# Two slots for the result instead of four, and a fourth chunk of slack in X and Y: a two-layer cross-head convolution on one Trainium2 core

## The chip, the cores and the metric

The kernel runs on one core of a Trainium2 chip. The metric is device time in microseconds of one execution, the median of several runs. The trace shows TensorE (PE, its weight loads as PEld), VectorE (DVE), ScalarE (ACT), GpSimd (POOL), SyncE (SP), which issues all DMAs here, and the DMA engines.

## The reference

```python
def layer(x, w, qw1, qw2, kw1, kw2, qdd, kdd):      # x: (1, 16, 1024, 1024), channels M, rows T, columns S
    ret = einsum('BGMTS,GMN->BGNTS', x, w + eye(16))
    ret += einsum('BGITS,BTGIM->BGMTS', einsum('BGMTS,BTGIM->BGITS', x, qw1), qw2)   # rank 2, by row t
    ret += einsum('BGITS,BSGIM->BGMTS', einsum('BGMTS,BSGIM->BGITS', x, kw1), kw2)   # rank 2, by column s
    return ret + x * qdd[by row] + x * kdd[by column]
out = layer(layer(x, *L0), *L1)
```

All is float32. At each point (t, s) the 16 channels are multiplied by a 16 x 16 matrix R[t] that depends on the row and by another C[s] that depends on the column, and the two products are added; this is done twice.

## The kernel before

**Layout.** The 1024 rows are cut into 8 blocks of 128 rows. A block of x lies on chip in X: a partition holds one channel of one eighth of the columns, and in it 64 pairs of rows by 128 columns by 2. Y is a second buffer of the same shape for what is between. A block is moved in 16 chunks of 8 rows, 512 KB each. X and Y are longer than a block by SLACK = 3 chunks: the blocks lie alternately at the start and at the end of the buffer (`pair_place`), so that the first three chunks of the next block (`pair_at`) have a place of their own, and each further chunk j of it takes the place of chunk j of the block before. OUT holds OUT_SLOTS = 4 chunks of the result.

**Matrices.** 16 x 16 matrices are spread to block-diagonal weights: those of rows from RT, of columns from RS. GpSimd makes all of WA and the odd groups of WB, VectorE the even groups of WB, each SLOTS = 4 groups ahead. The column matrices are made once at the start (`fill` on TensorE brings the factors to all partitions, `column_unit` on VectorE multiplies and adds). Their factors wait in KR: those of layer 0 in OUT, those of layer 1 in the slack of Y and X, one half each. The row matrices of the next block are made by VectorE in the T pass (`products_of`, at step PROD_STEP = 6), stored by SyncE (`store_products`, PROD_STORE = 9) and read back, broadcast, into RT.

**Passes.** Block k goes through an S pass and a T pass.

- S pass: TensorE multiplies by the column matrices, `s1` for layer 0 (out of X into the banks PB, which VectorE adds into Y: `add_columns`), `s2` for layer 1 (out of Y into PA, which ScalarE copies to X). VectorE starts an S pass only when ScalarE's copies of the T pass before are complete.
- T pass: for each of 16 steps o, TensorE multiplies a chunk of Y by the row matrices of layer 1 (`t2`, two groups, into PB) and then a chunk of the next block's x by the row matrices of layer 0 (`t1(k + 1, o)`, into PA, copied to Y by ScalarE). VectorE adds the part of PB and of X into OUT (`add_rows`, two a chunk, the first waits for the slot's last store), makes an even group of WB between the two adds, and makes the products behind step 6. `t2` takes the chunks in the order SLACK, SLACK + 1, ..., the first SLACK chunks last. The last block has no `t1`.

**Order on SyncE.** In a T pass it waits at each step for both adds, stores the chunk, and issues `load_x(k + 1, o + SLACK)`, whose place is now free. At step 9 it then stores the products (two DMAs) and loads the row parameters of the block after (`load_q`), before it comes to the store of step 10. The first SLACK chunks of a block are loaded at the start of the S pass before, ahead of the two loads of RT.

TensorE's `t1(k + 1, o)` needs chunk o of x landed; `t2` of group g needs the adds of group g - 4 (four banks PB) and its weights.

Of the kernel before, what the change touches and what calls it, by code (L numbers as in the profile page):

```python
# [10 lines left out]
EIGHTHS = HALVES * PARTS  # L11
# [4 lines left out]
RANK = 2  # L16
LAYERS = 2
PAIR = 2
PAIRS = ROWS // PAIR
CHUNK = 8  # L20
CHUNKS = ROWS // CHUNK
CHUNK2 = CHUNK // PAIR
SLACK = 3
NARROW = 4
GROUPS = WIDE // NARROW
INDEX = HALVES * NARROW
# [3 lines left out]
T2_GROUPS = ROWS // FEW  # L30
RING = 2
SLOTS = 4
OUT_SLOTS = 4
LAG = 2
QUARTERS = 4
QUARTER = COLS // QUARTERS
UNITS = LAYERS * QUARTERS * RANK
FILLS = 4
# [4 lines left out]
DMA = 16  # L43
FLAT = CHUNK * COLS
BANK = 512
# [5 lines left out]
def cross_conv_kernel(nc, x, first_rows, row_params, col_left, col_right, w, products, out):  # L51
# [13 lines left out]
    with ctx:  # L65
        def sb(name, shape):
            return ctx.enter_context(nc.sbuf_tensor(name, shape, f32))

        def sem(name):
            return ctx.enter_context(nc.semaphore(name))  # L70

        ALL = PAIRS + SLACK * CHUNK2
        X = sb("X", [P, ALL, COLS, PAIR])
        Y = sb("Y", [P, ALL, COLS, PAIR])
        OUT = sb("OUT", [P, OUT_SLOTS, CHUNK2, COLS, PAIR])
        RT = sb("RT", [P, LAYERS, ROWS, CH])
# [20 lines left out]
        sel = later[:, at:at + P]  # L97

        VALUES = RANK * COLS * CH
        KR = [[OUT[0:EIGHTHS, :, :, :, :].rearrange("q a b c d -> q (a b c d)")[:, 0:VALUES]],  # L100
              [buf[0:EIGHTHS, PAIRS:ALL, :, :].rearrange("q a b c -> q (a b c)")[:, 0:VALUES // 2]
               for buf in (Y, X)]]


        PA = [ctx.enter_context(nc.psum_tensor(f"PA{i}", [P, BANK], f32)) for i in range(RING * HALVES)]
        PB = [ctx.enter_context(nc.psum_tensor(f"PB{i}", [P, BANK], f32)) for i in range(RING * HALVES)]
# [1 line left out]
        x_loaded = [sem(f"x_loaded{j}") for j in range(CHUNKS)]  # L108
        first_loaded = sem("first_loaded")
        left_loaded = sem("left_loaded")  # L110
        right_loaded = [sem(f"right_loaded{h}") for h in range(3)]
        q_loaded = sem("q_loaded")
        ident_step = sem("ident_step")
        ident_ready = sem("ident_ready")
# [20 lines left out]
        b_done = sem("b_done")  # L135
        stored = [sem(f"stored{n}") for n in range(OUT_SLOTS)]

# [10 lines left out]
        def t2_groups(k):  # L148
            return (GROUPS + T2_GROUPS) * k + GROUPS
# [18 lines left out]
        def pair_place(k):  # L168
            return SLACK * CHUNK2 * (k % 2)

        def pair_at(k, j):

            if j >= SLACK:
                return CHUNK2 * j
            return CHUNK2 * j + PAIRS * (k % 2)

        def t2_chunk(o):
            return (o + SLACK) % CHUNKS

        def first(k):  # L180
            return isinstance(k, int) and k == 0
# [39 lines left out]
        def _(sp):  # L221
            def load_x(k, j):
                sp.dma_start(rows_of(X, k, j).rearrange("q a s c -> q (a s c)"),
                             x[bass.ds(k * CHUNKS + j, 1)].rearrange("b q v -> (b q) v")).then_inc(x_loaded[j], DMA)

            def store(k, o):
                sp.dma_start(out[bass.ds(k * CHUNKS + t2_chunk(o), 1)].rearrange("b q v -> (b q) v"),
                             OUT[:, o % OUT_SLOTS].rearrange("q a s c -> q (a s c)")
                             ).then_inc(stored[o % OUT_SLOTS], DMA)

            def load_right(l, h, signal):
                n = VALUES // len(KR[l])
                sp.dma_start(KR[l][h], col_right[l, :, n * h:n * (h + 1)]).then_inc(signal, DMA)

            def load_q(step):
                sp.dma_start(QP[:, :, :].rearrange("q l v -> q (l v)"),
                             row_params[bass.ds(step, 1)].rearrange("b t v -> (b t) v")).then_inc(q_loaded, DMA)

            def store_products(place, src, signal):
                sp.dma_start(products[bass.ds(place, 1)].rearrange("b c t n -> (b t) c n"), src).then_inc(signal, DMA)  # L240
# [7 lines left out]
            def s_phase(k, more):  # L248
                if more:
                    if not first(k):  # L250
                        sp.wait_ge(b_done, s1_done(k))
                    else:
                        sp.wait_ge(right_done, UNITS)
                    for j in range(SLACK):
                        load_x(k + 1, j)
# [13 lines left out]
            def t_phase(k, more, params):  # L269
                for o in range(CHUNKS):  # L270
                    sp.wait_ge(b_done, t2_done(k) + PER_CHUNK * (o + 1))
                    store(k, o)
                    if more and o + SLACK < CHUNKS:
                        load_x(k + 1, o + SLACK)
# [5 lines left out]
                            load_q(k + 2)  # L280

            sp.dma_start(QF, first_rows).then_inc(first_loaded, DMA)
            load_right(0, 0, right_loaded[0])
            sp.dma_start(KL.rearrange("q l i s -> q (l i s)"), col_left).then_inc(left_loaded, DMA)
            sp.dma_start(WI.rearrange("q l n -> q (l n)"),
                         w.unsqueeze(0).broadcast_to([EIGHTHS, CH, LAYERS * CH])).then_inc(left_loaded, DMA)
            load_x(0, 0)
            sp.wait_ge(first_prod, 1)
            store_products(BLOCKS * LAYERS, PF[:, 0], first_stored)
            for h in range(2):  # L290
                load_right(1, h, right_loaded[1 + h])
            load_q(0)
            load_x(0, 1)
            sp.wait_ge(first_stored, DMA)
# [18 lines left out]
            for slot in stored:  # L313
                sp.wait_ge(slot, DMA * BLOCKS * CHUNKS // OUT_SLOTS)

# [124 lines left out]
        def _(dve):  # L440
# [73 lines left out]
            def add_rows(k, g):  # L514
                o, inner = g // PER_CHUNK, FEW2 * (g % PER_CHUNK)
                dve.wait_ge(b_full, t2_groups(k) + g + 1)
                if g % PER_CHUNK == 0 and not (first(k) and o < OUT_SLOTS):

# [55 lines left out]
        def _(pe):  # L574
# [10 lines left out]
            def fill(u):  # L585

                l, place = u // (QUARTERS * RANK), u % (QUARTERS * RANK)
                per = QUARTERS * RANK // len(KR[l])
                pe.wait_ge(right_loaded[l + place // per], DMA)
                if u >= FILLS:  # L590
                    pe.wait_ge(right_done, u - FILLS + 1)
                nc.tensor.matmul(PB[u % FILLS][:, :], sel[0:EIGHTHS],  # L592
                                 KR[l][place // per][:, BANK * (place % per):BANK * (place % per + 1)],
                                 start=True, stop=True).then_inc(right_full, 1)

            def t1(k, j):
# [65 lines left out]
            for u in range(FILLS):  # L662
                fill(u)
            for j in range(CHUNKS):
                t1(0, j)
                if FILLS + j < UNITS:
                    fill(FILLS + j)
# [66 lines left out]
```

## Time and profile before

| | us |
|---|---|
| median of 3 runs | 865.64 |
| lowest, highest | 861.66, 874.1 |
| the profiled execution | 858.88 |
| its span, first to last instruction | 857.1 |
| busy: TensorE, its weight loads | 766.5, 704.4 |
| busy: VectorE, GpSimd, ScalarE | 546.1, 513.6, 393.6 |
| x loads, stores of the result (512 KB each) | 128, 128 |

The profile is of one execution. An engine's busy time is the sum over its instructions; a wait is idle time of an engine, put down to what released it. Times of rows count from the span's start. The mean granted clock of TensorE was 0.976 of full speed.

### The profile page before, as it was taken

What the parts mean: (1) busy time and instruction counts of PE and PEld (TensorE: products, weight loads), DVE (VectorE), ACT (ScalarE), POOL (GpSimd) and SP (SyncE); (2) the same over time, 40 slices, a digit from 0 to 9 for tenths busy, and PEclk for the clock granted to TensorE, in tenths of its full rate; (3) what the DMA queues carried; (4) which work ended last, traced back from release to release, by engine and by line L of the source; (5) the groups of instructions that cost most, each with busy time, mean ns of one, the idle gap of its engine ahead of it and who ended that gap; (6) DMA issues with size and microseconds to landing.
All of it is one profiled execution on the core that took longest, in us unless ns stands there. A gap on an engine that the chain in (4) does not pass through costs nothing.

```text
span 857.1 us, 42054 instructions
## 1 busy us (share of the span) xinstructions
PE 766.5 (89%) x18464; PEld 704.4 (82%) x18464; DVE 546.1 (64%) x809; ACT 393.6 (46%) x673; POOL 513.6 (60%) x456
## 2 busy tenths in 40 slices
PE   5998899799898999797998899979998889988998
PEld 2658799699787988797987898868998779877997
DVE  3338557468474866665676675837758566665668
ACT  6224563247432583225833466325743267324640
POOL 2326577467665677555766567646776567765733
PEclk9999999999999999989999999999999999999999
DMA  9804318952568618774098723785167840985026
GB/s 190 296 3 100 93 59 309 295 185 66 200 213 296 180 25 293 232 282 101 3 333 237 265 75 131 277 277 183 44 245 257 297 110 6 341 251 184 4 116 278
DMA packets 76045, 157.09 MB, mean 183 GB/s; under 512 B 39768, under 2 KB 40792, under 8 KB 73944
## 3 DMA queue, kind: packets, MB, share of 16 engines
q1 hardware_dynamic: 75888, 154.61, 55.5%
q8 instruction: 146, 2.39, 1.1%
q14 instruction: 11, 0.09, 0.0%
HBM read 85.25 MB, written 69.34 MB: 180 GB/s over the span
## 4 chain that ended last, share of the span: by engine, by line
POOL 34%; PE 25%; issue 24%; DVE 7%; DMA 5%; SPq 2%; POOLq 1%; ACT 1%; DVEq 0%; ACTq 0%
POOL WA L200 19%; POOL WB L208 9%; PE PB L655 7%; PE PA L607 7%; POOL WB L200 6%; PE PA L642 5%; PE PB L624 4%; DMA X<-in_x_dram 3%; DVE OUT L524 3%; PE PB L592 3%; DVE WB L208 2%; SPq L240 1%; DVE PROD L478 1%; DMA RT<-products 1%; DVE PROD L481 1%
## 5 line engine op out<-in xcount | busy, mean ns | idle before, releaser
L524 DVE TENSOR_TENSOR OUT<-PB,X 128x512 f32<-128x512 f32 x256 | 172.4, 686 | 185.0 <-PE PB L655 141.0
L402 ACT ACTIVATE Y<-PA 128x512 f32<-128x512 f32 (+1 forms) x256 | 147.3, 634 | 306.7 <-PE PA L607 306.7
L412 ACT ACTIVATE X<-PA 64x512 f32 (+3 forms) x384 | 232.7, 606 | 118.5 <-PE PA L642 111.8
L655 PE MATMUL PB<-Y,WB 128*128 128x128 f32 x2048 | 272.6, 286 | 1.7 <-issue 1.0
L655 PEld LDWEIGHTS PB<-Y,WB 128*128 128x128 f32 x2048 | 248.8, 193 | 15.8 <-issue 6.2
L208 POOL TENSOR_TENSOR WB<-RT,mask 128x512 f32<-128x512 f32 x128 | 156.3, 1221 | 106.1 <-PE PB L655 102.6
L511 DVE TENSOR_TENSOR Y<-PB,Y 128x512 f32 (+1 forms) x256 | 164.8, 685 | 80.7 <-PE PB L624 69.5
L607 PEld LDWEIGHTS PA<-X,WA 64*64 64x64 f32 x8192 | 149.4, 145 | 78.1 <-issue 37.8
L642 PE MATMUL PA<-Y,WA 64*64 64x128 f32 x4096 | 190.9, 311 | 20.7 <-issue 14.3
L607 PE MATMUL PA<-X,WA 64*64 64x64 f32 x8192 | 170.1, 234 | 44.0 <-DMA X<-in_x_dram 25.3
L200 POOL TENSOR_TENSOR WA<-RS,mask 128x512 f32<-128x512 f32 x128 | 139.4, 1089 | 110.7 <-PE PA L642 85.4
L624 PE MATMUL PB<-X,WB 64*64 64x128 f32 x4096 | 189.1, 311 | 14.6 <-DVE Y L511 9.3
L200 POOL TENSOR_TENSOR WA<-RT,mask 128x512 f32<-128x512 f32 x128 | 140.6, 1102 | 85.4 <-PE PA L607 47.1
L642 PEld LDWEIGHTS PA<-Y,WA 64*64 64x64 f32 x4096 | 163.7, 139 | 25.7 <-issue 16.4
L624 PEld LDWEIGHTS PB<-X,WB 64*64 64x64 f32 x4096 | 162.2, 139 | 18.7 <-issue 18.4
L208 DVE TENSOR_TENSOR WB<-RT,mask 128x512 f32<-128x512 f32 x128 | 102.8, 803 | 0.0
L200 POOL TENSOR_TENSOR WB<-RS,mask 128x512 f32<-128x512 f32 x64 | 80.7, 1262 | 33.6 <-PE PB L655 16.7
L200 DVE TENSOR_TENSOR WB<-RS,mask 128x512 f32<-128x512 f32 x64 | 69.2, 1082 | 0.0
L501 DVE TENSOR_TENSOR PB<-PB,RT 128x512 f32<-128x512 f32 x16 | 11.2, 700 | 31.1 <-PE PB L592 31.0
L478 DVE TENSOR_TENSOR PROD<-QP 128x256 f32<-128x256 f32 x32 | 22.3, 735 | 0.0
L592 PE MATMUL PB<-OUT,RT 8*128 8x512 f32 x16 | 15.4, 1104 | 5.4 <-DMA OUT<-in_right_dram 5.4
L419 ACT ACTIVATE RS<-RT,delta 128x128 f32<-128x128 f32 x32 | 12.5, 574 | 4.6 <-DVE RT L559 4.6
(24 smaller groups left out, 62.4 us busy)
## 6 DMA issues: line engine op xcount, KB each, us to landing
X<-in_x_dram SPq DMA_DIRECT2D x128, 512.0 KB, 6.0
out_dram<-OUT SPq DMA_DIRECT2D x128, 512.0 KB, 4.5
RT<-products SPq DMA_DIRECT2D x15, 1024.0 KB
products<-PROD SPq DMA_DIRECT2D x16, 128.0 KB, 8.2
RT<-products SPq DMA_DIRECT2D x1, 768.0 KB
QP<-in_rows_dram SPq DMA_DIRECT2D x8, 80.0 KB, 3.5
RT<-in_left_dram SPq DMA_DIRECT2D x1, 384.0 KB
RT<-products SPq DMA_DIRECT2D x1, 256.0 KB
```

Of the source, the lines that this page charges most:

```text
L200: engine.tensor_tensor(dst.rearrange("q (t a n) -> q t a n", t=CHUNK, a=PARTS), r, m, ALU.mult).then_inc(ready, 1)
L208: engine.tensor_tensor(dst.rearrange("q (t p n) -> q t p n", t=FEW, p=EIGHTHS), r, m, ALU.mult).then_inc(ready, 1)
L402: nc.scalar.activation(rows_of(Y, k, j)[:, :, WIDE * h:WIDE * (h + 1), :].rearrange("q a s c -> q a c s"), PA[HALVES * (j % RING) + h][:, ...
L412: nc.scalar.activation(columns_of(block_of(X, k), dst, WIDE * i + NARROW * g), by_columns(PA[HALVES * (g % RING) + i][src, :]), ACT.Copy). ...
L478: nc.vector.tensor_tensor(prod[:, i], q1[i].unsqueeze(2).broadcast_to(shape), q2[i].unsqueeze(1).broadcast_to(shape), ALU.mult).then_inc(p ...
L511: nc.vector.tensor_tensor(at, by_columns(PB[HALVES * (g % RING) + h][:, :]), at, ALU.add).then_inc(b_done, 1)
L524: nc.vector.tensor_tensor(rows(OUT[:, o % OUT_SLOTS]), PB[g % SLOTS][:, :].rearrange("q (a c s) -> q a c s", a=FEW2, c=PAIR), rows(rows_of ...
L592: nc.tensor.matmul(PB[u % FILLS][:, :], sel[0:EIGHTHS], KR[l][place // per][:, BANK * (place % per):BANK * (place % per + 1)], start=True, ...
L607: last = nc.tensor.matmul(PA[HALVES * (j % RING) + h][part(o), WIDE * r:WIDE * (r + 1)], matrix(WA[:, j % SLOTS], h, r), rows_of(X, k, j)[ ...
L624: last = nc.tensor.matmul(PB[HALVES * (g % RING) + h][part(o), ROWS * v:ROWS * (v + 1)] .rearrange("q (a c) -> q a c", c=PAIR), matrix(WB[ ...
L642: last = nc.tensor.matmul(PA[HALVES * (g % RING) + i][part(h ^ i), ROWS * v:ROWS * (v + 1)] .rearrange("q (a c) -> q a c", c=PAIR), matrix ...
L655: last = nc.tensor.matmul(PB[g % SLOTS][:, COLS * r:COLS * (r + 1)], WB[:, g % SLOTS, P * r:P * (r + 1)], rows_of(Y, k, t2_chunk(o))[:, (i ...
```

## The change

SLACK goes from 3 to 4 and OUT_SLOTS from 4 to 2. So X and Y are 4 KB a partition longer each, and OUT is 8 KB shorter. Four chunks of the next block have a place of their own, and step o of a T pass loads chunk o + 4. The first add of a chunk waits for the store of two chunks before. The factors of the column matrices lie whole in the slack of X (layer 0) and of Y (layer 1) and are loaded by one DMA each.

```diff
-SLACK = 3
+SLACK = 4
...
-OUT_SLOTS = 4
+OUT_SLOTS = 2
...
-        KR = [[OUT[0:EIGHTHS, :, :, :, :].rearrange("q a b c d -> q (a b c d)")[:, 0:VALUES]],
-              [buf[0:EIGHTHS, PAIRS:ALL, :, :].rearrange("q a b c -> q (a b c)")[:, 0:VALUES // 2]
-               for buf in (Y, X)]]
+        KR = [buf[0:EIGHTHS, PAIRS:ALL, :, :].rearrange("q a b c -> q (a b c)")[:, 0:VALUES] for buf in (X, Y)]
...
-        right_loaded = [sem(f"right_loaded{h}") for h in range(3)]
+        right_loaded = [sem(f"right_loaded{l}") for l in range(LAYERS)]
...
-            def load_right(l, h, signal):
-                n = VALUES // len(KR[l])
-                sp.dma_start(KR[l][h], col_right[l, :, n * h:n * (h + 1)]).then_inc(signal, DMA)
+            def load_right(l):
+                sp.dma_start(KR[l], col_right[l]).then_inc(right_loaded[l], DMA)
...
-            load_right(0, 0, right_loaded[0])
+            load_right(0)
...
-            for h in range(2):
-                load_right(1, h, right_loaded[1 + h])
+            load_right(1)
...
-                per = QUARTERS * RANK // len(KR[l])
-                pe.wait_ge(right_loaded[l + place // per], DMA)
+                pe.wait_ge(right_loaded[l], DMA)
...
-                                 KR[l][place // per][:, BANK * (place % per):BANK * (place % per + 1)],
+                                 KR[l][:, BANK * place:BANK * (place + 1)],
```

## Rows read from the trace of the kernel before

**Rows 1.** The page: busy time of each engine, its share of the span, instructions

```profile
PE 766.5 (89%) x18464; PEld 704.4 (82%) x18464; DVE 546.1 (64%) x809; ACT 393.6 (46%) x673; POOL 513.6 (60%) x456
```

**Rows 2.** Waits, whole run: engine, line, releaser: sum in us, times, longest

```profile
DVE OUT L524 <- PE PB L655: 141.0, 75, 7.9
...
PE PA L607 <- DMA X<-in_x_dram: 25.3, 14, 4.9
```

**Rows 3.** Busy time by stretch, T(4) and T(7); last: clock, DMA share, GB/s

```profile
522.20:585.70 63.50, 54.85 (x1348) 50.98 (x1345) 37.31 (x59) 20.84 (x36) 38.85 (x34) 0.97 0.73 248
821.70:857.10 35.40, 31.20 (x260) 29.65 (x256) 29.58 (x46) 2.37 (x4) 14.84 (x14) 1.00 0.59 238
```

**Rows 4.** Timeline of PE, T(4): start, us, line, operation, count, idle before

```profile
562.11 1.17 PE L607 MATMUL PA<-X,WA 64*64 64x64 f32 x64 [0.70 <-DMA X<-in_x_dram]
...
573.65 1.50 PE L607 MATMUL PA<-X,WA 64*64 64x64 f32 x64 [3.72 <-DMA X<-in_x_dram]
575.09 3.30 PE L655 MATMUL PB<-Y,WB 128*128 128x128 f32 x16
...
585.72 1.39 PE L624 MATMUL PB<-X,WB 64*64 64x128 f32 x32 [0.81 <-DVE Y L511]
```

**Rows 5.** Timeline of PE, x waits of T(0), T(3) and T(6)

```profile
169.13 1.99 PE L607 MATMUL PA<-X,WA 64*64 64x64 f32 x64 [4.93 <-DMA X<-in_x_dram]
...
459.12 1.17 PE L607 MATMUL PA<-X,WA 64*64 64x64 f32 x64 [0.29 <-DMA X<-in_x_dram]
...
770.16 1.17 PE L607 MATMUL PA<-X,WA 64*64 64x64 f32 x64 [1.20 <-DMA X<-in_x_dram]
```

**Rows 6.** Timeline of SyncE's issues in T(4), steps 9 and 10

```profile
557.09 0.35 SPq L227 DMA_DIRECT2D out_dram<-OUT  x1
557.64 0.75 SPq L223 DMA_DIRECT2D X<-in_x_dram  x1
558.68 5.83 SPq L240 DMA_DIRECT2D products<-PROD  x2
...
566.87 0.35 SPq L227 DMA_DIRECT2D out_dram<-OUT  x1
```

**Rows 7.** Landings in T(4): store 7; store 10; load 13; stores 11 to 13

```profile
DMA to landing us min/median/max: 2.9/2.9/2.9
...
DMA to landing us min/median/max: 3.2/3.2/3.2
...
DMA to landing us min/median/max: 6.2/6.2/6.2
...
DMA to landing us min/median/max: 6.8/7.9/8.4
```

**Rows 8.** Timeline of VectorE in T(7), two weight builds two chunks apart

```profile
844.09 0.95 DVE L208 TENSOR_TENSOR WB<-RT,mask 128x512 f32<-128x512 f32 x1
...
847.99 0.95 DVE L208 TENSOR_TENSOR WB<-RT,mask 128x512 f32<-128x512 f32 x1
```

**Rows 9.** Landings of the 16 stores of T(7)

```profile
DMA to landing us min/median/max: 2.6/2.7/3.7
```

**Rows 10.** Timeline of VectorE in T(4): adds of chunks 7, 12 and 15

```profile
550.60 0.68 DVE L524 TENSOR_TENSOR OUT<-PB,X 128x512 f32<-128x512 f32 x1
...
564.53 0.69 DVE L524 TENSOR_TENSOR OUT<-PB,X 128x512 f32<-128x512 f32 x1 [2.10 <-PE PB L655]
...
581.96 0.71 DVE L524 TENSOR_TENSOR OUT<-PB,X 128x512 f32<-128x512 f32 x1
```

**Rows 11.** Landings: store 7 of T(5); stores 7 and 10 of T(6)

```profile
DMA to landing us min/median/max: 5.1/5.1/5.1
...
DMA to landing us min/median/max: 4.6/4.6/4.6
...
DMA to landing us min/median/max: 5.0/5.0/5.0
```

**Rows 12.** Landings of all 128 stores

```profile
DMA to landing us min/median/max: 2.6/4.5/10.0
```

More of the change, by code:

```diff
@@ L587, in fill @@
                 l, place = u // (QUARTERS * RANK), u % (QUARTERS * RANK)
-                per = QUARTERS * RANK // len(KR[l])
-                pe.wait_ge(right_loaded[l + place // per], DMA)
+                pe.wait_ge(right_loaded[l], DMA)
                 if u >= FILLS:
                     pe.wait_ge(right_done, u - FILLS + 1)
-                nc.tensor.matmul(PB[u % FILLS][:, :], sel[0:EIGHTHS],
-                                 KR[l][place // per][:, BANK * (place % per):BANK * (place % per + 1)],
+                nc.tensor.matmul(PB[u % FILLS][:, :], sel[0:EIGHTHS], KR[l][:, BANK * place:BANK * (place + 1)],
                                  start=True, stop=True).then_inc(right_full, 1)
```

## The prediction

> **What bounds the kernel now.** I read the page's busy shares first: TensorE is busy for 766.5 us of 857.1 [rows 1], so a change pays only where it removes idle time of TensorE, or shifts the few places where another engine ends last. The list of waits comes second. TensorE waits for loads of x for 25.3 us in 14 waits [rows 2]; that sum is what the fourth chunk of slack can address. VectorE waits 141.0 us for TensorE in the T passes [rows 2], so in general it has spare time there, and a new wait on it costs only what exceeds that.
>
> Third comes the table by stretch. I write T(k) for the T pass of block k. In T(4), 522.2 to 585.7 us, VectorE is busy 37.31 of 63.5 us and the DMA engines 0.73 [rows 3]. In the last pass, T(7), which has no next block to interleave, VectorE is busy 29.58 of 35.4 us and TensorE 31.20 [rows 3]: there the two are level and neither has room.
>
> Fourth, the timeline of TensorE. Each of T(0) to T(6) has at most two sizeable x waits: before t1 of chunk 10, 0.70 us in T(4), and before t1 of chunk 13, 3.72 us in T(4) [rows 4]; over the passes single waits run from 0.29 us (T(3), chunk 10) to 4.93 us (T(0), chunk 13) [rows 5]; the seven at chunk 10 sum to 7.1 us, the rest stands at chunk 13 and, 0.75 us in T(6), at chunk 14. After the long one the granted clock is at its lower level (1.2 instead of 2.4 GHz): the next two groups take 1.50 and 3.30 us in place of 1.17 and 2.08, 1.55 us more [rows 4].
>
> Fifth, SyncE's issues say why chunk 13. With SLACK 3, load 12 goes out behind store 9 at 557.64, then the two stores of products take SyncE's queue for 5.83 us from 558.68, and store 10, with load 13 behind it, comes at 566.87 [rows 6]. Load 13 lands 6.2 us after its issue [rows 7], some 573.6, exactly when TensorE goes on.
>
> **Part 1: four chunks of slack.** Load 10 now follows store 6 instead of store 7, so it no longer sits behind VectorE's products (step 6), and that wait goes. Load 13 now follows store 9 and goes out before the products, about 8.5 us before TensorE asks; that wait goes too. What is late next is load 14: it takes the place of load 13 behind store 10. Its landing, 6.2 us after issue, is when TensorE arrives one chunk (3.1 us) later, so a wait is left, from 0.1 us in T(4) to 1.3 us in T(0). The same 128 loads and 128 stores are made, each of 512 KB. Four of a block's loads instead of three go out at the start of its S pass, ahead of the RT loads; the DMA engines have room there, and RT is wanted tens of us later, so this costs nothing. If that cover were gone, it would be one load, about 1.5 us a block. The factors of layer 0 and 1 load into X and Y slack, as one DMA each: same bytes, and the first is waited for as before; nothing. Another order of the row chunks inside the pass changes no shape; nothing.
>
> **Part 2: two slots for OUT.** VectorE's first add of chunk o now waits for store o-2 where it waited for store o-4. Behind the waiting add stand on VectorE: the even WB weights of two chunks ahead, for which TensorE waits, then the second add, whose completion SyncE wants before store o and load o+4.
>
> In T(7) the sum is clear. VectorE spends 1.95 us a chunk (from its weight build at 844.09 to the like one at 847.99 are two chunks, 3.9 us) [rows 8]. A store lands 2.6 us after issue at the least, median 2.7, most 3.7 [rows 9]. A slot's round is then: two adds and a weight build 2.0, to the issue 0.1, landing 2.6, to the add 0.1: 4.8 us for two chunks instead of 3.9. That is 0.45 us a chunk, for 14 chunks 6.3 us; the first two stores land slower (up to 3.7), so I take **+6.5 us**, bounds 5 (some of it absorbed by what lies after the last add) and 10 (3.1 us a landing throughout). No cover exists here: the pass ends the kernel.
>
> The Trainium skill's main page, section Best Practices, says to double-buffer so that DMA and compute overlap. Taken as it stands, two slots would do and T(7) would cost nothing, the sum 6.5 us lower; the landing of 2.6 us against 1.95 us of work a chunk speaks against that. Its page "DMA: Bandwidth & Descriptors", section Anatomy of one DMA, fits about 2.0 us plus bytes over 436 GB/s per DMA (measured there on another issue path), an estimated 3.2 us for 512 KB, by which T(7) would lose 0.75 us a chunk, 10 us; the trace here has 2.6.
>
> In T(0) to T(6) I walk T(4). Chunks 0 to 6: stores land up to 6 us after issue behind the loads, so VectorE begins chunks 2 to 4 up to 2 us late, but TensorE needs the even weights only two chunks later and VectorE has 1 us spare in each chunk of 3.1; by step 6 it is level. Products occupy it until 550.60 [rows 10]. It then catches up at 2 us a chunk. Store 7 lands 2.9 us after 552.65 [rows 7], at 555.6, where the first add of chunk 9 ran at 554.9: +0.7. Store 9 and all behind it, the products too, move by 0.7: store 10 at 567.6, landed (3.2 us [rows 7]) at 570.8. Only then may chunk 12 be added (564.5 before), so the weights for t2 of chunk 14 are ready at 572.2. TensorE, without its x waits, arrives at 570.3 and waits 1.9 us. Stores 11 to 13 took 6.8 to 8.4 us [rows 7]; store 11 lands at 575.5, weights for chunk 15 at 576.9, TensorE waits another 1.4 and starts the S pass at 580.1, where it was 582.4: 2.3 us won. But VectorE's last adds hang on stores 12 and 13 (landed 578.1 and 580.7), and end at 582.7, as before (581.96 + 0.71 [rows 10]). The S pass's third group waits for VectorE's column adds, 585.72 before [rows 4]; now 584.2. So T(4) wins **1.5 us** of the 4.4 + 1.5 that stood there: the store chain replaces the load wait.
>
> The other passes go by the same steps; what differs is the landing of store 7, which sets how late chunk 9 and the products start, that of store 10, and the x wait that goes. T(6), the worst: store 7 lands 4.6 us after its issue at 751.69, chunk 9 starts 2.8 us late, store 10 moves from 763.7 to 766.4 and lands after 5.0 us [rows 11] at 771.4, weights for chunk 14 at 772.8 where t2 began at 771.3; the x wait won was only 1.20 [rows 5], and VectorE ends 2.3 us later: +2.3. T(5): store 7 lands after 5.1 us [rows 11], 2.9 us late, +1.0. T(0), the best: 0.9 us late, and 4.93 us of wait go [rows 5]; load 14 and store 13 hold the end: -2.4. Between them T(1) -0.4, T(2) +1.1 (it had no wait at chunk 13 to win) and T(3) +0.7. Sum of seven: **+0.8 us**. Bounds: -3 a pass (-21), if stores land in 2.6 us as in T(7), and +2.2 a pass (+15), if in 5 us or more.
>
> **Sum.** 0.8 + 6.5 = 7.3 us on the profiled execution's 858.88, 866.2. That execution lies 6.8 us under the median of the runs, 865.64, which I take as base: 865.64 + 7.3 = 872.9, rounded **872**.
>
> **Rivals.** (a) *Slower: the store chain rules every T pass.* Place: VectorE before the first add of chunks 9, 12 and 14. Price: if stores behind loads land in over 4.1 us (two chunks of 3.11 less 2.1 of work and issue), VectorE falls behind by half of the excess each chunk; the median over all passes is 4.5 us and the most 10.0 [rows 12]. It then reaches products late and every pass ends some 2.3 us later: 7 x 2.3 + 8 = 24, time 889. For it: the median is above the point. Against: those landings are backlog, and a later issue lands sooner. (b) *The x waits go whole and stores don't bite in the middle*: -25.3, and 6 to 7 of half clock (1.55 where it fell), + 6.5 in T(7): -25, time 841. For it: VectorE's 141.0 us of waiting. Against: store 10 is stuck behind the products whatever the slack. (c) *Two slots suffice everywhere*, the double-buffering rule: T(7) costs nothing, T passes win the 1.5 of T(4) each: -10, time 855. Against: 4.8 over 3.9 us. (d) *It doesn't do what it says*: the wait of chunk 13 moves whole to chunk 14, only chunk 10's 7 us are won: 0 with T(7), time 865.
>
> **How the numbers follow.** About 2% (17 us, 848 to 883) is what a measurement here tells from none; the runs before alone span 861.66 to 874.1. Forecast 0.55, (a) 0.18, (b) 0.05, (c) 0.10, (d) 0.12. Faster by over 2% is (b): 0.05. Slower is most of (a) and the edge of the forecast: 0.18. Within: 0.77. The range goes from (c) with 3 us of scatter, 852, to (a), 888.
>
> **What would show it.** Right: VectorE waits on "DMA out_dram<-OUT" at chunks 9, 12 and 14; T(7) longer by 6 to 7 us; TensorE's x waits under 10 us, what is left at chunk 14; TensorE waiting for WB weights of VectorE at chunk 14. Wrong: x waits of 20 us or more at chunk 14, T(7) at 31 us again, or TensorE waiting for VectorE's weights at chunks 4 to 9. Most likely cause of a miss: landings of stores when fewer loads stand before them, which no row shows.

## The result, and the profile after

The changed kernel took 883.83 us (median of 4 runs, 880.39 to 884.28) against 863.65 us before (4 runs, 856.28 to 874.1): ratio 1.0254, 95% interval 1.0178 to 1.0331. It is slower, by 20 us in the medians; whether by more than 2% the interval leaves open. The ratios and their intervals leave out runs that lie over 1.5% above the fastest of the same kernel, the medians don't (without them before has 861.66 us, and the difference is 22 us). The profiled execution has a span of 882.3 us where before had 857.1, so 25.2 us are to be found in the traces.

The list of waits of the changed kernel (engine, line, releaser: sum in us, times, longest):

```profile
DVE OUT L520 <- DMA out_dram<-OUT: 138.9, 76, 6.5
...
PE PB L649 <- DVE WB L206: 43.2, 25, 3.3
...
PE PB L618 <- DVE OUT L520: 13.9, 10, 3.5
DVE OUT L520 <- PE PB L649: 11.8, 8, 2.0
...
PE PA L601 <- DMA X<-in_x_dram: 0.5, 2, 0.3
```

The slack does what it is for: TensorE's waits for x go from 25.3 [rows 2] to 0.5 us. But VectorE, which waited 141.0 us for TensorE [rows 2], now waits 138.9 us for stores and 11.8 for TensorE: the order of who leads is turned round. What TensorE won on x it lost more than once over, 43.2 us on VectorE's weights and 13.9 on its adds.

Where the 25.2 us lie, from the timelines of TensorE (a T pass from its first t2 matmul to the first s2 matmul of the S pass behind it, an S pass from there to the next t2):

| us | before | after | difference |
|---|---|---|---|
| T(0) to T(6) | 63.9, 65.3, 63.7, 61.0, 64.6, 60.6, 59.4 = 438.5 | 60.7, 63.3, 65.4, 64.8, 63.5, 68.7, 62.6 = 449.0 | +10.5 |
| T(7), TensorE's part | 31.1 | 39.1 | +8.0 |
| seven S passes | 263.8 | 268.8 | +5.0 |
| start, and from the last matmul to the end | 119.4 + 4.2 | 119.9 + 5.6 | +1.9 |

(The first S pass lies in the start. The rows are rounded, so they sum to 25.4; T(0) to T(6) after are 448.9 unrounded.)

What fills T(0) to T(6), as sums of idle time in TensorE's timelines: waits for weights 0.7 us before and 36.6 after, for VectorE's adds into OUT 0 and 13.9, for its column adds 5.4 and 0, for x 25.3 and 0.5, and stalls of TensorE's own, which the rows call "issue", 15.3 and 5.3. The busy time is 391.7 and 392.3 us.

The timeline of TensorE in T(4) of the changed kernel:

```profile
550.96 2.08 PE L649 MATMUL PB<-Y,WB 128*128 128x128 f32 x16
552.98 1.17 PE L601 MATMUL PA<-X,WA 64*64 64x64 f32 x64
557.46 3.78 PE L649 MATMUL PB<-Y,WB 128*128 128x128 f32 x16 [3.32 <-DVE WB L206]
561.17 1.99 PE L601 MATMUL PA<-X,WA 64*64 64x64 f32 x64
...
581.45 2.08 PE L649 MATMUL PB<-Y,WB 128*128 128x128 f32 x16 [0.63 <-DVE WB L206]
583.46 1.17 PE L601 MATMUL PA<-X,WA 64*64 64x64 f32 x64
584.44 1.38 PE L618 MATMUL PB<-X,WB 64*64 64x128 f32 x32
587.16 2.59 PE L618 MATMUL PB<-X,WB 64*64 64x128 f32 x64 [1.34 <-DVE OUT L520]
```

The big wait is no longer at chunk 13 for x [rows 4] but at chunk 9 for weights, 3.32 us, and behind it the granted clock is at its lower level again (3.78 and 1.99 us where 2.08 and 1.17 stand at the upper): 2.5 us more. The wait stands at chunk 9 in T(1), T(3), T(4) and T(6) with 3.32 us each, in T(5) with 1.74: 15.0 us in five passes. VectorE in the same pass says why:

```profile
533.85 0.69 DVE L520 TENSOR_TENSOR OUT<-PB,X 128x512 f32<-128x512 f32 x1 [1.49 <-DMA out_dram<-OUT]
534.46 1.58 DVE L206 TENSOR_TENSOR WB<-RT,mask 128x512 f32<-128x512 f32 x1
...
545.32 0.69 DVE L520 TENSOR_TENSOR OUT<-PB,X 128x512 f32<-128x512 f32 x1 [2.44 <-DMA out_dram<-OUT]
...
548.75 0.69 DVE L520 TENSOR_TENSOR OUT<-PB,X 128x512 f32<-128x512 f32 x1 [1.54 <-DMA out_dram<-OUT]
...
550.55 1.98 DVE L474 TENSOR_TENSOR PROD<-QP 128x256 f32<-128x256 f32 x2
...
556.12 0.69 DVE L520 TENSOR_TENSOR OUT<-PB,X 128x512 f32<-128x512 f32 x1
556.73 0.68 DVE L206 TENSOR_TENSOR WB<-RT,mask 128x512 f32<-128x512 f32 x1
...
575.37 0.69 DVE L520 TENSOR_TENSOR OUT<-PB,X 128x512 f32<-128x512 f32 x1 [4.72 <-DMA out_dram<-OUT]
```

Chunks 2, 3, 5 and 6 wait for stores (chunk 3 for 1.62 us at 538.26), so the products begin 24.5 us into the pass (550.55 less 526.04) and end at 556.1; the weights for chunk 9 are made at 556.73 to 557.4, and TensorE, there at 554.1, goes on at 557.46. The same places in T(4) of the kernel before, which starts at 522.25, first on TensorE, then on VectorE:

```profile
538.63 0.58 PE L607 MATMUL PA<-X,WA 64*64 64x64 f32 x22 [1.00 <-issue]
...
549.06 0.45 PE L607 MATMUL PA<-X,WA 64*64 64x64 f32 x11 [0.65 <-issue]
...
552.55 2.08 PE L655 MATMUL PB<-Y,WB 128*128 128x128 f32 x16
```

```profile
545.28 1.86 DVE L478 TENSOR_TENSOR PROD<-QP 128x256 f32<-128x256 f32 x2
...
551.20 0.68 DVE L208 TENSOR_TENSOR WB<-RT,mask 128x512 f32<-128x512 f32 x1
```

There the products began 23.0 us into the pass, and the weights for chunk 9 were ready at 29.6 us (551.9), now at 31.4. TensorE comes earlier: to chunk 9 at 30.3 us before (552.55) and at 28.1 now. In one pass before, T(1), the weights of chunk 9 were late already:

```profile
251.23 2.08 PE L655 MATMUL PB<-Y,WB 128*128 128x128 f32 x16 [0.66 <-DVE WB L208]
```

Later, chunk 12 waits 4.72 us for store 10, which was again behind the products on SyncE:

```profile
563.71 0.35 SPq L225 DMA_DIRECT2D out_dram<-OUT  x1
564.25 0.35 SPq L221 DMA_DIRECT2D X<-in_x_dram  x1
564.89 4.71 SPq L237 DMA_DIRECT2D products<-PROD  x2
569.79 1.89 SPq L233 DMA_DIRECT2D QP<-in_rows_dram  x1
571.94 0.35 SPq L225 DMA_DIRECT2D out_dram<-OUT  x1
```

T(7), TensorE's timeline: what was one unbroken stretch of 31.15 us is now cut by waits for weights.

```profile
837.59 7.79 PE L649 MATMUL PB<-Y,WB 128*128 128x128 f32 x64
846.15 3.90 PE L649 MATMUL PB<-Y,WB 128*128 128x128 f32 x32 [0.78 <-DVE WB L206]
851.85 3.90 PE L649 MATMUL PB<-Y,WB 128*128 128x128 f32 x32 [1.80 <-DVE WB L206]
856.51 3.90 PE L649 MATMUL PB<-Y,WB 128*128 128x128 f32 x32 [0.76 <-DVE WB L206]
861.17 3.90 PE L649 MATMUL PB<-Y,WB 128*128 128x128 f32 x32 [0.77 <-DVE WB L206]
867.55 9.14 PE L649 MATMUL PB<-Y,WB 128*128 128x128 f32 x64 [2.48 <-DVE WB L206]
```

From 856.51 to 861.17 are two chunks, 4.66 us: the round of one slot (2.0 of work, 2.6 of landing and a little between), where two chunks of work alone are 3.9. The 8.0 us that the pass is longer are the five waits, 6.6 us in sum, and half clock behind the last of them: the four chunks from 867.55 take 9.14 us where the four from 837.59 take 7.79.

### The profile page after: what moved, and what is told of

The parts are those of the page before. It is cut to its first block, busy times and chain, and to the rows that moved or that the text cites. A ratio compares the mean times of both kernels' runs of the same rounds, so it can differ in the third digit from the quotient of the medians.

```text
span 882.3 us, 42083 instructions
## 1 busy us (share of the span) xinstructions
PE 771.3 (87%) x18464; PEld 708.1 (80%) x18464; DVE 567.1 (64%) x809; ACT 393.9 (45%) x673; POOL 512.8 (58%) x456
## 4 chain that ended last, share of the span: by engine, by line
PE 40%; DMA 19%; DVE 15%; issue 11%; POOL 6%; SPq 4%; ACT 3%; DVEq 1%; ACTq 0%; POOLq 0%
DMA out_dram<-OUT 17%; PE PB L618 13%; PE PA L636 12%; PE PB L649 7%; PE PA L601 6%; DVE OUT L520 5%; DVE WB L206 5%; POOL WA L198 4%; ACT X L408 3%; DVE PROD L474 3%; PE PB L587 3%; SPq L237 2%; POOL WB L198 2%; DVE PROD L477 1%; SPq L233 1%
## 5 line engine op out<-in xcount | busy, mean ns | idle before, releaser
L649 PE MATMUL PB<-Y,WB 128*128 128x128 f32 x2048 | 273.5, 286 | 43.4 <-DVE WB L206 43.2
L520 DVE TENSOR_TENSOR OUT<-PB,X 128x512 f32<-128x512 f32 x256 | 173.4, 686 | 194.7 <-DMA out_dram<-OUT 138.9
L206 POOL TENSOR_TENSOR WB<-RT,mask 128x512 f32<-128x512 f32 x128 | 148.7, 1162 | 128.9 <-PE PB L649 125.4
L618 PE MATMUL PB<-X,WB 64*64 64x128 f32 x4096 | 195.3, 316 | 25.5 <-DVE OUT L520 13.9
L198 POOL TENSOR_TENSOR WA<-RS,mask 128x512 f32<-128x512 f32 x128 | 143.1, 1118 | 90.0 <-PE PA L636 81.9
L618 PEld LDWEIGHTS PB<-X,WB 64*64 64x64 f32 x4096 | 168.2, 143 | 30.5 <-issue 26.8
L636 PEld LDWEIGHTS PA<-Y,WA 64*64 64x64 f32 x4096 | 167.5, 141 | 26.0 <-issue 16.7
L198 POOL TENSOR_TENSOR WA<-RT,mask 128x512 f32<-128x512 f32 x128 | 144.6, 1134 | 74.1 <-PE PA L601 33.4
L206 DVE TENSOR_TENSOR WB<-RT,mask 128x512 f32<-128x512 f32 x128 | 117.6, 919 | 0.0
L474 DVE TENSOR_TENSOR PROD<-QP 128x256 f32<-128x256 f32 x32 | 27.2, 891 | 0.0
L587 PE MATMUL PB<-X,RT 8*128 8x512 f32 x16 | 15.4, 1104 | 5.3 <-DMA X<-in_right_dram 5.3
L587 PE MATMUL PB<-Y,RT 8*128 8x512 f32 x16 | 16.5, 1136 | 0.0
```

Of the source, the lines that this page charges most:

```text
L198: engine.tensor_tensor(dst.rearrange("q (t a n) -> q t a n", t=CHUNK, a=PARTS), r, m, ALU.mult).then_inc(ready, 1)
L206: engine.tensor_tensor(dst.rearrange("q (t p n) -> q t p n", t=FEW, p=EIGHTHS), r, m, ALU.mult).then_inc(ready, 1)
L474: nc.vector.tensor_tensor(prod[:, i], q1[i].unsqueeze(2).broadcast_to(shape), q2[i].unsqueeze(1).broadcast_to(shape), ALU.mult).then_inc(p ...
L520: nc.vector.tensor_tensor(rows(OUT[:, o % OUT_SLOTS]), PB[g % SLOTS][:, :].rearrange("q (a c s) -> q a c s", a=FEW2, c=PAIR), rows(rows_of ...
L587: nc.tensor.matmul(PB[u % FILLS][:, :], sel[0:EIGHTHS], KR[l][:, BANK * place:BANK * (place + 1)], start=True, stop=True).then_inc(right_f ...
L618: last = nc.tensor.matmul(PB[HALVES * (g % RING) + h][part(o), ROWS * v:ROWS * (v + 1)] .rearrange("q (a c) -> q a c", c=PAIR), matrix(WB[ ...
```

## The experiments

Each time below is a median; the kernel before ran beside each experiment, with medians of 861.5 to 863.0 us. All edits are given against the kernel named.

**The four corners: two slots alone, slack alone.** The first leaves SLACK at 3 and uses two of the four slots; the kernel before with:

```diff
-OUT_SLOTS = 4
+OUT_SLOTS = 2
...
-        OUT = sb("OUT", [P, OUT_SLOTS, CHUNK2, COLS, PAIR])
+        OUT = sb("OUT", [P, 2 * OUT_SLOTS, CHUNK2, COLS, PAIR])
```

> SLACK stays 3, only two of the four OUT slots are used. Theory (store chain): the last pass grows from 31.1 to about 39 us as in the changed kernel, the passes with a next block keep their waits for x (20 us or more, since load 13 is still behind the products) and get the waits for weights on top, so the kernel is slower than the changed one: 885 to 900 us. Rival (the four chunks of slack cost, for example by more loads in the S pass): two slots alone cost only the last pass, 870 to 875 us.

893.72 us, ratio 1.0404 (1.0347 to 1.046). As the theory had it. Its waits for stores, x and weights:

```profile
DVE OUT L524 <- DMA out_dram<-OUT: 139.3, 78, 5.3
...
PE PA L607 <- DMA X<-in_x_dram: 39.0, 20, 5.5
...
PE PB L655 <- DVE WB L208: 19.9, 12, 3.3
```

The waits for x grow from 25.3 to 39.0 (by the order on SyncE a later add makes a later load), and 19.9 for weights come on top. T(7) is 38.3 us.

The second has both, SLACK 4 and four slots, on the changed kernel, with the room taken from RS:

```diff
-OUT_SLOTS = 2
+OUT_SLOTS = 4
...
-        RS = sb("RS", [P, LAYERS, COLS, CH])
+        RS = sb("RS", [P, 1, COLS, CH])
```

and all uses of `RS[:, 0]` and `RS[:, 1]` on that one half (ScalarE's base for layer 1 goes to the still unused OUT).

> SLACK 4 with four OUT slots; the room comes from RS, of which both layers use one half, so the column matrices of the second layer are not its own (same instructions, another result). Theory: waits for x fall from 25.3 to under 10 us (left at chunk 14, behind the products), the last pass is 31 us again, time 840 to 852 us. Rival (the slack is worth nothing, because the wait moves whole to chunk 14): x waits 18 us or more, time 855 to 865 us.

844.99 us, ratio 0.9833 (0.9779 to 0.9887). Waits for x:

```profile
PE PA L603 <- DMA X<-in_x_dram: 8.0, 6, 1.9
...
PE PB L651 <- DVE WB L206: 3.5, 6, 0.7
```

The time and the waits are as the theory had them. T(7) is 31.15 us again, T(0) to T(6) sum to 419.3. So with four slots the slack wins 16.5 us and with two 9.9 (893.72 less 883.83), while the two slots cost 32 with SLACK 3 and 39 with SLACK 4. The change is a win of some 10 to 16 us bought with 32 to 39.

**The products later on SyncE's queue.** One constant, on the kernel before (to 12) and on the changed one (to 15):

```diff
-PROD_STORE = 9
+PROD_STORE = 12
```

> The kernel before, with the two stores of products and the load of row parameters behind step 12 instead of 9, when all loads of x of the pass are out. Theory (SyncE's queue, held by the products, makes load 13 late): the waits for x at chunk 13 go, those at chunk 10 (7 us in sum) stay, time 840 to 852 us. Rival (the transfers themselves are late because the DMA engines are full): waits for x stay at 20 us or more, time 858 to 868 us.

> The changed kernel, with the stores of products behind step 15 instead of 9. Theory (in the passes with a next block, part of the loss is the store of chunk 10 held behind the products, then chunks 12 and 14): the waits of TensorE for weights late in the pass shrink, those at chunk 9 stay, the last pass stays at 39 us; time 866 to 876 us. Rival (two slots lag by themselves, whatever stands on SyncE's queue): 880 to 886 us.

841.3 us, ratio 0.9796 (0.9728 to 0.9863), and 863.7 us, ratio to before 1.005 (0.9986 to 1.0115): 20 us each. The first one's waits for x, and then the changed kernel's waits with the same edit:

```profile
PE PA L607 <- DMA X<-in_x_dram: 7.5, 9, 1.5
```

```profile
DVE OUT L520 <- DMA out_dram<-OUT: 105.4, 80, 3.2
...
PE PB L649 <- DVE WB L206: 25.3, 18, 3.3
```

So what made load 13 late was SyncE's queue, not full DMA engines: no x wait at chunk 13 is left, and the 7.5 us stand at chunks 10 and 11. One constant wins as much as the fourth chunk of slack (20 against 16.5 us, a difference within the intervals). In the changed kernel the same edit takes 18 of the 43 us of weight waits, mostly late in the passes; the 3.3 us at chunk 9 stay in four passes (243.61, 445.04, 542.49, 742.43 us in its timeline), T(7) is 37.8. The time, 863.7 us, is a little under what was expected.

**Both on the slack.** The kernel with SLACK 4 and four slots, PROD_STORE 12:

> SLACK 4, four OUT slots (both layers again on one half of RS, so another result) and the stores of products behind step 12. Theory (the slack is worth what load 13 and load 10 gain; late products alone already free load 13): only the chunk 10 wait of some 7 us is left for the slack to win over late products alone (841.3), time 832 to 838 us, x waits under 2 us. Rival (slack and late products add in full, -16.5 and -20): 825 us.

837.89 us, ratio 0.9673 (0.9583 to 0.9762). TensorE waits for x no more. Against late products alone, 841.3, the slack is worth 3 us, within the intervals of both: the two remedies treat the same wait and do not add.

**Four slots in the last pass alone.** The changed kernel; in T(7) chunks 2 and 3 of every four use X's free slack (the adds, the stores and their waits all go by `slot`):

```diff
+        def slot(k, o):
+            if last(k) and o % 4 >= 2:
+                n = o % 4 - 2
+                return X[:, CHUNK2 * n:CHUNK2 * (n + 1)], spare_stored[n]
+            return OUT[:, o % OUT_SLOTS], stored[o % OUT_SLOTS]
```

> The changed kernel, where the last pass alone takes two more slots, in the slack of X that no load uses then. Theory (a slot's round of work, issue and landing sets the last pass): it falls from 39.1 to 31 us, time 875 to 877 us. Rival (the last pass is longer for another reason, such as VectorE's slower weight builds beside GpSimd): it stays over 36 us, time 882 us or more.

878.16 us, ratio 1.0148 (1.007 to 1.0226). The time is a little over the 875 to 877 us of the theory. The last pass of it, one row again:

```profile
842.23 31.15 PE L664 MATMUL PB<-Y,WB 128*128 128x128 f32 x256
```

So the slots are the whole of the 8.0 us there. They are also the 1.4 us from the last matmul to the end, which is 4.2 us again: 9.4 us by the traces. The medians differ by 5.7; in the profiled pair T(0) to T(6) are as long (448.5 and 448.9 us) and the S passes 5.0 us longer, which is their scatter (below).

**The products in two pieces on VectorE.** On the kernel before with PROD_STORE 12, and, in steps 3 and 6 with the stores left behind step 9, on the changed one:

```diff
-                    if more and o == PROD_STEP:
-                        products_of(k + 1)
+                    if more and o in (3, 7):
+                        products_of(k + 1, ((0,), (1,))[o == 7])
```

> The kernel before with the stores of products behind step 12, and VectorE's products cut in two, layer 0 behind step 3 and layer 1 behind step 7. Theory (the remaining 7.5 us of x waits at chunk 10 come from VectorE being held 5.4 us in one piece behind step 6): they fall under 2 us, time 832 to 837 us. Rival (they come from the landing of loads under full DMA engines): unchanged, 841 us.

> The changed kernel with VectorE's products cut in two, layer 0 behind step 3 and layer 1 behind step 6, stores as before behind step 9. Theory (with two slots VectorE comes late into the products, so that the weights of chunk 9 are late, 15.7 us of TensorE's wait over the passes plus half clock): those waits halve or go, time 868 to 876 us. Rival (the lag is only moved, each piece of products meets the store chain): 880 us or more.

829.76 us, ratio 0.9609 (0.9536 to 0.9682): waits for x 1.4 us, and a time under what was expected; the waits at chunks 10 and 11 did come from VectorE being held in one piece behind step 6. And 871.18 us, ratio 1.0107 (1.0064 to 1.015), 12.7 under the changed kernel. The time is as the theory said, and so are the waits at chunk 9, which fall from 15.0 to 4.1 us. But others come in their place, as the rival had it, and the sum of all waits for weights hardly falls from 43.2:

```profile
PE PB L649 <- DVE WB L206: 41.9, 34, 4.4
```

There are now more and shorter ones (34 in place of 25), most of them of 0.6 to 0.8 us; the long ones left stand at chunk 14 (4.37 us in T(4)). T(0) to T(6) sum to 436.9, not 448.9; TensorE is busy in them for 384.7 us, not 392.3, and the mean granted clock of the run is 0.976, not 0.964. So some 7 of the 12 us are half clock that stood behind long waits. The sum of waits is not the price: one wait of 3.32 us with 2.5 us of half clock behind it costs more than five of 0.65.

**All on the changed kernel.** Late and split products; then also four slots in T(7); then also the fourth x load of an S pass late in it:

```diff
-                    for j in range(SLACK):
+                    for j in range(SLACK - 1):
...
+                    sp.wait_ge(a_full, s2_groups(k) + 10)
+                    load_x(k + 1, SLACK - 1)
```

> The changed kernel with both: products of VectorE in two pieces (steps 3 and 6) and their stores behind step 15. Theory (in the passes with a next block the two slots cost time mainly where they meet the products, on VectorE and on SyncE's queue): the weight waits of those passes fall from 36.6 to under 12 us, the last pass stays near 38; time 850 to 856 us. Rival (two slots cost as much without the products): 862 us as with late stores alone.

> As the run before, and the last pass with two more slots in free slack. Theory (the parts add): 6 to 8 us less than the run before, 843 to 849 us, still over the kernel before with late and split products (829.8), since the slack then has little to win. Rival (the slack wins 10 us once nothing else holds the pass): 830 us or less.

> As the run with all three edits on the changed kernel (late and split products, four slots in the last pass), but of the four loads of x at the start of an S pass the fourth goes out late in that pass, behind ten of its sixteen groups. Theory (the fourth load beside the loads of RT lengthens TensorE's stalls on its own instruction fetch, so that the seven S passes sum to 267 to 281 us with SLACK 4 against 260 to 270 with SLACK 3): the sum falls to 270 or less, time 826 to 831 us. Rival (those sums differ by chance or for another reason): 274 us or more, time as before, 835.

849.74 us, ratio 0.9767 (0.9685 to 0.9849); 834.82 us, ratio 0.9646 (0.9581 to 0.9711); 835.32 us, ratio 0.9612 (0.9558 to 0.9665). One run of the last took 3443 us; that isn't explained.

The first is just under its range. Its weight waits are 16.3 us, 4.1 of them in T(7), so 12.2 in the other passes where under 12 were expected. T(0) to T(6) sum to 412.8 us there and, with the same code for these passes, to 406.0 in the second; four slots with late and split products have 405.3. So away from the products two slots cost these passes little, at most the 7 us by which the two traces differ.

The second came 15 us under the first by the medians, where 6 to 8 were expected, and under its range. But these medians have few runs that scatter: by the runs that the ratios count (838.36 and 847.07 us; 827.18, 834.27 and 835.38) they are 842.7 and 834.3, which is 8.4 us apart. The edit itself explains 7.9 by the traces: T(7) is 31.15 in place of 37.6, and from the last matmul to the end it is 4.2 in place of 5.6. The third tests a guess on the S passes: their sum is 280.3 us, as without the edit (281.4), and the time is as before; the theory falls.

**The best version once more.**

> Four slots, SLACK 3, products in two pieces (steps 3 and 7) and stored behind step 12, once more with more rounds: 826 to 834 us, 3 to 5% under the kernel before.

830.28 us, ratio 0.9652 (0.9598 to 0.9705), 6 runs: four slots, SLACK 3, products in two pieces and stored late. It has run twice, at 829.76 and 830.28. The changed kernel with all remedies, 834.8, is not ahead of it.

## Why the prediction was right or wrong

The time fell inside the range, above the value: 7.3 us were forecast, 20 came. The likeliest outcome, a change under 2%, had 0.77, and the ratio came out at 1.0254 with an interval that reaches below 1.02. That the time is in the range is owed to rival (a), which set its upper end. (865.64 and 7.3 are 872.9, so the rounded value would have been 873.) The signs that it named are mixed: the x waits are under 10 us and the waits at chunk 14 are there, but TensorE waits for VectorE's weights at chunk 9, which it had listed under "wrong". The sum, term by term:

- *Slack.* Right. The waits for x went, and the corner with four slots shows what is late next, loads behind the products (six waits, five of them at chunk 14, 8.0 us in sum, the longest 1.87); in the changed kernel hardly any is left (0.5 us), as TensorE comes late itself. A small misreading: the waits of T(4) (0.70 us) and T(6) (0.36) that it put at chunk 10 stand at chunk 11; their sum, and what the slack does to them, are the same.
- *T(7), +6.5.* Mechanism right, the term under by 1.5: 8.0 measured. The round of 4.8 was right (4.66), and so was the sum of waits, 6.6 us, in which rounds of 4.66 stand beside longer ones where a store landed late (up to 4.4 us) or a weight build took 1.26 us. What the term lacked is the half clock behind the last wait, 1.35 us, and the end: the last matmul to the end takes 1.4 us more. With it two slots cost the pass 9.4 us, near the upper bound of 10. Four slots in that pass alone give both back.
- *T(0) to T(6), +0.8.* Measured +10.5, and this is the step that failed: "by step 6 it is level". VectorE was to catch up by 1 us a chunk, but in T(4) the stores of chunks 3 and 4 held chunks 5 and 6 again (2.44 and 1.54 us), VectorE reached the products 1.5 us later than before, and the weights of chunk 9 came 3.3 us after TensorE. The walk had TensorE's chunks 4 to 9 as T(4) of the trace before has them, where TensorE lost 1.00 and 0.65 us to stalls of its own issue in t1 of chunks 4 and 7, and so came to t2 of chunk 9 only 0.7 us after its weights were ready. Without those stalls it would have come a us early even then; in T(1) of that trace TensorE did wait there, for 0.66 us. The cover was this pass's alone. In T(4) the weight waits at chunks 14 and 15, forecast at 1.9 and 1.4, were 0.64 and 0.63, since the pass had already waited at chunk 9. Nor did I charge the new wait with the half clock behind it, though [rows 4] has it for the old one: 2.5 us in T(4). With all else left as it is, splitting the products takes 11 of the 15.0 us at chunk 9 away and brings these passes to 436.9 us, 1.6 under before.
- *The same, pass by pass.* Forecast were -2.4, -0.4, +1.1, +0.7, -1.5, +1.0 and +2.3; measured are -3.2, -2.0, +1.7, +3.7, -1.1, +8.1 and +3.2. That T(1), T(4) and T(6) come out near the forecast is luck: each has the wait of 3.32 us that was not forecast, and each lost stalls of TensorE's own that were not counted as a gain (2.0 to none, 3.4 to 0.8, 1.9 to 0.2 us). T(5) alone is 7 us over: 8.1 us of waits for weights at chunks 9, 11, 14 and 15, and 3.5 us for the adds behind them.
- *S passes, 0.* +5.0 in the profiled pair. Over all traces the seven S passes sum to 260 to 270 us in the five with SLACK 3 and to 266 to 281 in the nine with SLACK 4. The three highest of these, 280 to 281 us, are from executions 8 to 11 us over their kernels' medians; without them it is 266 to 274, which overlaps. So part or all of it may be scatter. Delaying the fourth load did not lower the sum, so the reason given in that experiment falls; if there is a cost, its cause is open.

Rival (a), that the store chain rules the T passes, priced 24 us; it is what the measured 20 lie nearest to, but its place was off: chunks 9, 12 and 14, yes, by way of chunks 2 to 6, which it named only in its point of 4.1 us. Rival (b), a gain in the middle, needs four slots: it is the corner at 845, without the cost in T(7). Rival (c), that two slots suffice, and with it the double-buffering rule of the Trainium skill taken as it stands, is out: they cost 32 us. Rival (d), that the wait moves whole to chunk 14, is out: with four slots 8.0 of the 25.3 us are left.

## What to carry to other kernels

A buffer's slots are sized by its round, work + issue + landing, over the work of one chunk, at the place where the consumer has no room; an average of 141 us of idle time says nothing about that, since the same idle time was cover for the transfers. Before memory is spent on running loads further ahead, look at what stands before the late load on its queue: moving two small stores and a small load by three steps won 20 us, as much as the slack's 16.5 within the intervals, and cost no memory. Where a step "catches up by" some point, check it with the other stalls of the pass taken out, and price a new wait with the clock that it may cost.

## What the runs showed of the hardware

VectorE's identical weight build costs more where its place in time has moved. The groups of before and after (mean ns of one behind the busy time):

```profile
L208 DVE TENSOR_TENSOR WB<-RT,mask 128x512 f32<-128x512 f32 x128 | 102.8, 803 | 0.0
```

```profile
L206 DVE TENSOR_TENSOR WB<-RT,mask 128x512 f32<-128x512 f32 x128 | 117.6, 919 | 0.0
```

Over all traces the mean is 803 to 824 ns in the six that have four slots in all passes and 874 to 922 ns in the eight with two. GpSimd's timeline beside the build of 1.58 us at 534.46:

```profile
534.44 1.06 POOL L206 TENSOR_TENSOR WB<-RT,mask 128x512 f32<-128x512 f32 x1 [0.76 <-PE PB L649]
```

Both engines started within 0.02 us of each other, and VectorE's build lasted 1.06 + 0.5 us. The Trainium skill's page "SBUF — State Buffer", section "SBUF: two separate sides", says that VectorE and GpSimd share a pair of ports which one instruction holds whole while the other waits. The row agrees; no run here took the overlap away by itself, so as a cause it is argued, not shown. Nor does a run separate how much of the loss in T(0) to T(6) is these dearer builds (117.6 less 102.8, 15 us of VectorE's time) and how much the waits for stores.

A long wait of TensorE is often followed by half clock, but not always. In the changed kernel the group behind 3.32 us took 3.78 us at 557.46, the one behind 2.48 us in T(7) has it too, and in T(0) the same group behind 3.27 us took 2.08:

```profile
169.20 2.08 PE L649 MATMUL PB<-Y,WB 128*128 128x128 f32 x16 [3.27 <-DVE WB L206]
```

TensorE's own stalls ("issue") are fewer where it waits for VectorE: in T(0) to T(6) they sum to 15 to 21 us in the six traces with four slots in all passes and to 1 to 8 us in the eight with two. So part of a new wait is paid back by stalls that go; why, no run shows.
